# One of 31 gathered chunks of a graph layer loaded row by row by SyncE and ScalarE

## Chip, cores and metric

One core of one Trainium2 chip. The metric is the device time of one execution in microseconds, the median of three runs.

## What is computed

The input is `x`, 6250 nodes of 256 features, and 200000 edges sorted by their destination, with a weight each. A normalised `xn` goes through three branches that are summed: two graph convolution layers and a projection, a linear attention with its own feed-forward part, and then, on the sum, a mixture of eight experts of which each node takes two.

```python
def _gcn_conv(x, edge_index, edge_weight, W, b):
    deg = segment_sum(ew, col); dis = rsqrt(deg)            # with self-loops of weight 1
    h = x @ W.T
    msg = h[row] * (dis[row] * ew * dis[col])[:, None]
    return segment_sum(msg, col) + b

xn = layernorm(x)
x = x + gnn(xn, edges) + mix(xn)      # gnn: two blocks x + relu(gcn(layernorm(x))), then x @ Wp.T + bp
x = x + ffn(layernorm(x))             # 8 experts, top 2
```

What matters here is `h[row]` summed by `col`: for each destination node, the rows of `h` of all its edges' source nodes.

## The kernel before

The nodes are cut into 49 windows of 128 (`W`), the sorted edges into chunks of 128. A window needs the edges of at most a few dozen chunks; it takes 31 of its own (`OWN`), one shared with the window before it (its 31st slot is reused for that), and, in a loop whose count is only known at run time, any that are left over ("rest", about one a window). For each chunk the kernel needs two tiles: `gs[:, n, :]`, 128 rows of the table `h1_d` in HBM (layer 1) or `h2_d` (layer 2), one for each edge, at 1 KB a row; and `ss[:, slot, :]`, a 128 x 128 matrix made by VectorE that has an edge's weight in the column of its destination. The TensorE sums `ss.T @ gs` over the chunks into one PSUM bank (`acc`).

There are three stages: a preparation (degrees, normalisation, the table h1; to about 250 us in the trace), the loop of layer 1 over 49 windows (`window1` on each engine), and the loop of layer 2 (`window2`), in which the experts are computed as well. In both loops the engines run their own programs and meet at semaphores:

- GpSimd (`gathers`, `chunks`) issues one indirect DMA for each chunk (line 521). It takes 128 indices from `idx_all[:, w, n]` (partition e holds the source node of edge e) and loads the rows into `gs[:, n, :]`. Ahead of it stands a wait on `main_used` (line 520), by which the same slot's use in the window before is over. It issues `chunks(w, 8..30)`, then `chunks(w + 1, 0..7)`, then the rest of w (line 530). Each chunk has a semaphore `main_in{n}`.
- TensorE (`messages`) takes eight groups of four chunks a window (k = 0 to 7) and waits for `main_in` of each. Between the groups it does a step of the attention branch and the transposes: with k = 0 the product with `wq`, with k = 2 `nd` and a transpose of z, with k = 3 a transpose and `next_h`, with k = 4 the product with `wm`, with k = 5 a transpose, with k = 6 the 32 products of the hidden layer, with k = 7 a transpose and the product with `w2`.
- ScalarE copies what TensorE puts in PSUM back to SBUF for TensorE's next step: in order `xT` (line 646), the exponential (648), `xn_keep` (650), the weights of an expert (652), `zT` (636, `next_h`), `mT` (657), `u4` (641, `next_h_scaled`), `nT` (660), and four activations into `hT` (664).
- VectorE makes the `ss` tiles (line 1038) and does the layer norms; line 1089 is one of its once-a-window instructions.
- SyncE moves whole tiles of 128 KB: in order `ew_in` (365), `hself` (367), `u2` (369), `u1` (372), the stores of h2 (374), x1 (376) and r (384), each behind the semaphore of the instruction that it follows.

Where an engine uses a table's value as an address or a loop's bound, it reads it from SBUF into a register by `value_load` (`lookup`, line 269); before the change VectorE, TensorE and GpSimd do so.

Of the kernel before, what the change touches and what calls it, by code (L numbers as in the profile page):

```python
# [24 lines left out]
P = 128  # L25
# [9 lines left out]
S_SLOTS = 16  # L35
EARLY = (8, 16)
LO_MIN = 1
DEG = OWN + 5
PACK = 4
FRONT = 8  # L40
# [50 lines left out]
def gps_kernel(nc, x, src_cols, dst_cols, ew_cols, dst_rows, vecs, W6T, W7T, WpT, Wq, Wk, Wv, Wm, W1, W2,  # L91
               ln_cols, mix_cols, Wg, bg, eW, eb1, eb2, out):
    with ExitStack() as ctx:
# [195 lines left out]
            return lookup(eng, T_DN, w, 1, NCOL), lookup(eng, T_DBASE, w, 0, W * NCOL)  # L289

        @block.sync
        def _(sp):

# [55 lines left out]

            sp.wait_ge(s["blank_out"], 16 * 6)
            sp.wait_ge(s["kv_acc"], W)
            sp.wait_ge(s["h1_out"], 16 * (W // XG + 1))
            for b in range(2):
# [4 lines left out]
            def window1(w, last=False):  # L360
# [9 lines left out]
                sp.wait_ge(s["xn1_tp"], w + 1)  # L370
                sp.wait_ge(s["xn_kept"], w + 1)
                sp.dma_start(u1[:, :], xn_d[bass.ds(after, P), :]).then_inc(s["xn_in"], 16)
                sp.wait_ge(s["h2_done"], w + 1)
                sp.dma_start(h2_d[bass.ds(here, P), :], u4[:, :]).then_inc(s["h2_out"], 16)
                sp.wait_ge(s["x1_done"], w + 1)
                sp.dma_start(x1_d[bass.ds(here, P), :], u5[:, :]).then_inc(s["x1_out"], 16)
                if last:
# [48 lines left out]
        def _(pool):  # L426
# [82 lines left out]
            def gathers(layer, table):  # L509
                pool.wait_ge(s[f"table{layer + 1}"], 1)  # L510

                def chunks(w, some):
                    g = layer * W + w
                    for n in some:
                        if layer == 0 and n == 0:
                            pool.wait_ge(s["idx_listed"], w + 1)
                        if n == OWN - 1:
                            pool.wait_ge(s["main_used"], g * STATIC + 1 + S_SLOTS)
                        elif g:
                            pool.wait_ge(s["main_used"], (g - 1) * STATIC + n + 2 + S_SLOTS)  # L520
                        pool.indirect_dma_start(  # L521
                            gs[:, n, :], None, table[:, :],
                            bass.IndirectOffsetOnAxis(ap=idx_all[:, w, n:n + 1], axis=0),
                            element_offset=P * D).then_inc(s[f"main_in{n}"], 16)
# [23 lines left out]
        def _(act):  # L548
# [91 lines left out]
                act.wait_ge(s["h2_out"], 16 * w)  # L640
                act.activation(u4[:, :], wide(7), ACT.Copy, scale=dis[:, bass.ds(w, 1)]).then_inc(s["h2_done"], 1)

            with act.Fori(0, W) as w:
                act.wait_ge(s["xn1_tp"], w + 1)
                act.wait_ge(s["hh_ps"], w)
                act.copy(xT[:, :, :], half(5)).then_inc(s["xn1T_set"], 1)
# [1 line left out]
                act.activation(t_a[1][:, :], t_a[0][:, :], ACT.Exp).then_inc(s["q_exp"], 1)  # L648
                act.wait_ge(s["x1_done"], w)
                act.copy(xn_keep[:, :], u1[:, :]).then_inc(s["xn_kept"], 1)  # L650
                act.wait_ge(s["experts_in"], 16 * (w + 1))
                act.activation(ew_part[0][:, bass.ds(w * EW_STEP, EW_STEP)], ew_in[:, :], ACT.Copy,
                               scale=W_UP).then_inc(s["ew_high"], 1)
                next_h(w)
                act.wait_ge(s["msg_tp"], w + 1)
                act.wait_ge(s["m_ps"], w)
                act.copy(mT[:, :, :], half(5)).then_inc(s["msgT_set"], 1)
                next_h_scaled(w)
                act.wait_ge(s["mn_tp"], w + 1)
                act.copy(nT[:, :, :], half(5)).then_inc(s["mnT_set"], 1)  # L660
                act.wait_ge(s["hh_ps"], w + 1)
                act.wait_ge(s["y1_ps"], w)
                for j in range(HBLK):
                    act.activation(hT[0][:, j, :], bank[6][:, j * P:(j + 1) * P], ACT.Relu,  # L664
                                   bias=w1bias[:, j:j + 1]).then_inc(s["hr_done"], 1)
            next_h(W)
            next_h_scaled(W)

# [601 lines left out]
        def _(pe):  # L1270
# [127 lines left out]
            def messages(turn, v, k, fresh=False):  # L1398
# [1 line left out]

                pe.wait_ge(s["main_set"], v + k * U + U)
                for q in range(k * U, k * U + U):
                    if q:
                        pe.wait_ge(s[f"main_in{q - 1}"], 16 * (turn + 1))
                    mm(acc, ss[:, q % S_SLOTS, :], gs[:, q - 1 if q else OWN - 1, :], fresh and q == 0, True,
                       skip_group_check=True).then_inc(s["main_used"], 1)
# [213 lines left out]
```

## Time and profile before

| | |
|---|---|
| median of three runs | 6317.9 us (6287.8 to 6318.42) |
| span of the profiled execution | 4375.4 us |
| mean granted TensorE clock | 0.914 |
| TensorE busy | 3602.6 us, 82% |
| GpSimd busy | 3096.7 us, 71% |
| VectorE busy | 2502.6 us, 57% |
| ScalarE busy | 1195.2 us, 27% |
| indirect transfers | 3038 of `gs`, 116 of `gr` |
| moved by DMA | 515.38 MB, mean 118 GB/s |

The span runs from the first to the last instruction of one profiled execution; its durations are what the rows below give. The time of a run is not the span: 1942.5 us lie between them, and the profile has no row for these.
### The profile page before, as it was taken

Reading aid. Unit: us, or ns where it says so; the run is one execution under the profiler, and the core shown is the slowest. Engines: PE = TensorE matmul, PEld = TensorE weight load, DVE = VectorE, ACT = ScalarE, POOL = GpSimd, SP = SyncE. Lnnn points to the kernel's source line nnn. Section 1 sums busy time; section 2 is a strip of 40 time slices with the busy share of each in tenths; the row PEclk is TensorE's granted clock in tenths of the full one; section 3 lists DMA queues with packets and bytes.
Section 4 is the critical chain, followed back from the end, with each engine's and each line's share of the span. In section 5 each row is a group of like instructions: output and inputs, shape, how many; then the busy total and the mean of one; then the engine's idle time right before and its main releaser. Section 6 shows DMA issues by size and latency. Waiting matters only on the chain.

```text
span 4375.4 us, 93734 instructions
## 1 busy us (share of the span) xinstructions
PE 3602.6 (82%) x26676; PEld 3057.6 (70%) x26677; DVE 2502.6 (57%) x8948; ACT 1195.2 (27%) x3161; POOL 3096.7 (71%) x3340
## 2 busy tenths in 40 slices
PE   5976766766776776767778999999999999999989
PEld 4855655655655655655657888888888887888878
DVE  8854555554554554544555665665666565665655
ACT  2520100100110110101113444444444444444434
POOL 3357777777777777777767777777777777777772
PEclk9988888888888888888889999999999999999999
DMA  4144444444444444444433343443344343343331
GB/s 150 50 139 119 129 126 124 129 126 119 131 129 119 130 130 119 130 123 126 127 111 116 112 117 115 115 118 115 112 117 118 111 117 115 115 118 115 115 111 53
DMA packets 256046, 515.38 MB, mean 118 GB/s; under 512 B 61480, under 2 KB 154032, under 8 KB 255984
## 3 DMA queue, kind: packets, MB, share of 16 engines
q0 software_dynamic: 151392, 413.60, 33.2%
q1 hardware_dynamic: 104592, 101.17, 6.9%
q14 instruction: 49, 0.40, 0.0%
q8 instruction: 13, 0.21, 0.0%
HBM read 474.81 MB, written 39.71 MB: 118 GB/s over the span
## 4 chain that ended last, share of the span: by engine, by line
PE 48%; DVE 14%; issue 12%; POOL 11%; DMA 7%; ACT 4%; DVEq 2%; SPq 1%; POOLq 0%; ACTq 0%
PE bank L1282 46%; POOL gs L521 11%; DMA gr<-h_d,idx_r 7%; DVE ss L1038 2%; PE bank L1304 2%; ACT L696 1%; DVE rstd L717 1%; DVE rstd L715 1%; DVE rstd L716 1%; DVE st L724 1%; ACT bank L696 1%; DVEq L269 1%; DVE w L1179 1%; ACT w L699 1%; DVEq L1038 1%
## 5 line engine op out<-in xcount | busy, mean ns | idle before, releaser
L521 POOL DMA_INDIRECT gs<-h_d,idx_all x3038 | 2902.3, 955 | 957.5 <-issue 659.4
L1282 PE MATMUL bank<-gs,ss 128*128 128x256 f32 x6272 | 1601.5, 402 | 12.3 <-DMA gs<-h_d,idx_all 12.3
L1282 PEld LDWEIGHTS bank<-gs,ss 128*128 128x128 f32 x6272 | 1219.9, 202 | 191.7 <-DMA gs<-h_d,idx_all 23.2
L1038 DVE TENSOR_SCALAR ss<-iw,dst_all,ew 128x128 f32<-128x128 f32 x3152 | 882.9, 354 | 183.8 <-PE bank L1282 125.8
L696 ACT ACTIVATE bank<-bank,eb1c 128x128 f32<-128x128 f32 x1616 | 448.8, 340 | 634.3 <-PE bank L1282 633.8
L1282 PE MATMUL bank<-experts,w 128*128 128x256 f16 x4848 | 605.3, 278 | 16.8 <-DVE w L1179 16.8
L1282 PE MATMUL bank<-w,experts 128*128 128x128 f16 x9696 | 608.4, 220 | 0.0
L1282 PEld LDWEIGHTS bank<-w,experts 128*128 128x128 f16 x9696 | 569.0, 98 | 44.4 <-issue 16.6
L1282 PEld LDWEIGHTS bank<-experts,w 128*128 128x128 f16 x4848 | 468.4, 100 | 91.1 <-issue 22.1
L1282 PE MATMUL bank<-gr,sr 128*128 128x256 f32 x232 | 115.6, 593 | 479.2 <-DMA gr<-h_d,idx_r 479.2
L1179 DVE SCALAR_TENSOR_TENSOR w<-bank,w 128x512 f16<-128x512 f32 x404 | 278.3, 689 | 360.9 <-ACT w L699 360.4
L1282 PEld LDWEIGHTS bank<-gr,sr 128*128 128x128 f32 x232 | 49.2, 261 | 525.0 <-DMA gr<-h_d,idx_r 524.5
L1122 DVE SCALAR_TENSOR_TENSOR t_b<-bank,dis,vec 128x256 f32<-128x256 f32 x49 | 23.7, 484 | 490.4 <-PE bank L1282 490.4
L648 ACT ACTIVATE t_a<-t_a 128x256 f32<-128x256 f32 x49 | 20.4, 416 | 993.2 <-DVE t_a L1086 993.2
L1173 DVE SCALAR_TENSOR_TENSOR u<-bank,mask_c,u 128x256 f32<-128x256 f32 x404 | 192.9, 478 | 141.6 <-PE bank L1282 138.9
L699 ACT ACTIVATE w<-bank 128x512 f16<-128x512 f32 x404 | 241.2, 597 | 12.8
L1304 PE MATMUL bank<-ident,u 128*128 128x128 f32 x596 | 121.0, 285 | 110.1 <-DVE u L733 101.6
L530 POOL DMA_INDIRECT gr<-h_d,idx_r x116 | 112.0, 965 | 116.3 <-DVE idx_r L1045 86.7
L1304 PEld LDWEIGHTS bank<-ident,u 128*128 128x128 f32 x596 | 76.0, 142 | 167.1 <-DVE u L733 121.7
L1045 DVE COPY idx_r<-src_row 128x1 int32 x116 | 17.8, 154 | 247.2 <-PE bank L1282 208.5
L664 ACT ACTIVATE hT<-bank,w1bias 128x128 f32<-128x128 f32 x196 | 55.9, 368 | 285.3 <-PE bank L1282 285.3
L1282 PE MATMUL bank<-xT,w 128*128 128x128 f32 x784 | 126.3, 286 | 0.0
(270 smaller groups left out, 3434.1 us busy)
## 6 DMA issues: line engine op xcount, KB each, us to landing
gs<-h_d,idx_all POOLq DMA_INDIRECT x3038, 2.7
hself<-h_d SPq DMA_DIRECT2D x100, 128.0 KB, 3.2
ew_in<-in_eW SPq DMA_DIRECT2D x49, 168.0 KB, 2.6
out<-u SPq DMA_DIRECT2D x51, 128.0 KB
u<-xn_d SPq DMA_DIRECT2D x50, 128.0 KB, 3.4
h_d<-u SPq DMA_DIRECT2D x50, 128.0 KB, 1.9
u<-x_d SPq DMA_DIRECT2D x50, 128.0 KB
u<-r_d SPq DMA_DIRECT2D x50, 128.0 KB, 2.8
```

What stands on the lines that cost most here:

```text
L269: return eng.value_load(tab[0:1, row, bass.ds(w, 1)], min_val=low, max_val=high)
L521: pool.indirect_dma_start(gs[:, n, :], None, table[:, :], bass.IndirectOffsetOnAxis(ap=idx_all[:, w, n:n + 1], axis=0), element_offset=P * ...
L530: pool.indirect_dma_start(gr[:, :], None, table[:, :], bass.IndirectOffsetOnAxis(ap=idx_r[:, 0:1], axis=0), element_offset=P * D).then_inc ...
L664: act.activation(hT[0][:, j, :], bank[6][:, j * P:(j + 1) * P], ACT.Relu, bias=w1bias[:, j:j + 1]).then_inc(s["hr_done"], 1)
L696: act.activation(hid[e % 2][:, j, :], hid[e % 2][:, j, :], ACT.Gelu, scale=1.0 / (Z_UP * W_UP), bias=eb1c[:, e, j:j + 1]).then_inc(s["gelu ...
L699: act.activation(hT_part[e % 2][0][:, :, :], hid[e % 2], ACT.Copy, scale=H_UP).then_inc(s["h_high"], 1)
L715: ch.link(dve.tensor_tensor(t, y, y, ALU.mult))
L1038: m = dve.tensor_scalar(ss[:, slot + j, :], iw[:, :], dst_f[:, bass.ds(c, 1)], ew[:, bass.ds(c, 1)], ALU.is_equal, ALU.mult)
L1173: dve.scalar_tensor_tensor(out=u8[:, :], in0=wide((7, 5)[e % 2]), scalar=mask_c[:, e:e + 1], in1=u8[:, :], op0=ALU.mult, op1=ALU.add).then ...
L1179: dve.scalar_tensor_tensor(out=hT_part[e % 2][1][:, :, :], in0=hid[e % 2], scalar=H_UP, in1=hT_part[e % 2][0][:, :, :], op0=ALU.mult, op1= ...
L1282: return pe.matmul(out_ap, lhsT, rhs, start=first, stop=last, **kw)
L1304: m = pe.transpose(half(b)[:, k, :], src[:, k * P:(k + 1) * P], ident[:, :])
```

## The change

In layer 1, for each window but the first, the chunk of slot 2 (`ROWS`) is no longer gathered by GpSimd. During window w, SyncE and ScalarE load its 128 rows for window w + 1 one at a time: for each edge a register load of the source node from `idx_all`, and a direct transfer of that 1 KB row of `h1_d` into its partition of `gs`. SyncE takes partitions 0 to 63, half behind the load of `u1` and half behind the store of h2. ScalarE takes 64 to 127, sixteen each behind `xn_keep`, behind `zT`, behind `u4` and behind the four activations. Both wait first until the slot's use in window w is over. All transfers add to one semaphore, `rows_by_hand`, and TensorE waits for it ahead of the fourth message of a window. ScalarE's loop runs over 48 windows now, with the last written out behind it; both engines wait for all 49 index lists ahead of their loops.

```diff
--- before.py
+++ after.py
@@ -35,6 +35,8 @@
 S_SLOTS = 16
 EARLY = (8, 16)
 LO_MIN = 1
+ROWS = 2
+BY_SP = P // 2
 DEG = OWN + 5
 PACK = 4
 FRONT = 8
@@ -288,6 +290,12 @@
         def degree_table(eng, w):
             return lookup(eng, T_DN, w, 1, NCOL), lookup(eng, T_DBASE, w, 0, W * NCOL)
 
+
+        def row_loads(eng, w, rows_of):
+
+            for p in rows_of:
+                node = eng.value_load(idx_all[p:p + 1, bass.ds(w + 1, 1), ROWS], min_val=0, max_val=N_NODES - 1)
+                eng.dma_start(gs[p:p + 1, ROWS, :], h1_d[bass.ds(node + P, 1), :]).then_inc(s["rows_by_hand"], 16)
 
         @block.sync
         def _(sp):
@@ -350,6 +358,7 @@
 
 
             sp.wait_ge(s["blank_out"], 16 * 6)
+            sp.wait_ge(s["idx_listed"], W)
             sp.wait_ge(s["kv_acc"], W)
             sp.wait_ge(s["h1_out"], 16 * (W // XG + 1))
             for b in range(2):
@@ -370,8 +379,13 @@
                 sp.wait_ge(s["xn1_tp"], w + 1)
                 sp.wait_ge(s["xn_kept"], w + 1)
                 sp.dma_start(u1[:, :], xn_d[bass.ds(after, P), :]).then_inc(s["xn_in"], 16)
+                if not last:
+                    sp.wait_ge(s["main_used"], w * STATIC + (ROWS + 2 + S_SLOTS))
+                    row_loads(sp, w, range(0, BY_SP // 2))
                 sp.wait_ge(s["h2_done"], w + 1)
                 sp.dma_start(h2_d[bass.ds(here, P), :], u4[:, :]).then_inc(s["h2_out"], 16)
+                if not last:
+                    row_loads(sp, w, range(BY_SP // 2, BY_SP))
                 sp.wait_ge(s["x1_done"], w + 1)
                 sp.dma_start(x1_d[bass.ds(here, P), :], u5[:, :]).then_inc(s["x1_out"], 16)
                 if last:
@@ -512,6 +526,8 @@
                 def chunks(w, some):
                     g = layer * W + w
                     for n in some:
+                        if layer == 0 and w and n == ROWS:
+                            continue
                         if layer == 0 and n == 0:
                             pool.wait_ge(s["idx_listed"], w + 1)
                         if n == OWN - 1:
@@ -640,7 +656,10 @@
                 act.wait_ge(s["h2_out"], 16 * w)
                 act.activation(u4[:, :], wide(7), ACT.Copy, scale=dis[:, bass.ds(w, 1)]).then_inc(s["h2_done"], 1)
 
-            with act.Fori(0, W) as w:
+            def window1(w, last=False):
+                by_act = [range(BY_SP + i * (P - BY_SP) // 4, BY_SP + (i + 1) * (P - BY_SP) // 4) for i in range(4)]
+                if last:
+                    by_act = [()] * 4
                 act.wait_ge(s["xn1_tp"], w + 1)
                 act.wait_ge(s["hh_ps"], w)
                 act.copy(xT[:, :, :], half(5)).then_inc(s["xn1T_set"], 1)
@@ -648,14 +667,19 @@
                 act.activation(t_a[1][:, :], t_a[0][:, :], ACT.Exp).then_inc(s["q_exp"], 1)
                 act.wait_ge(s["x1_done"], w)
                 act.copy(xn_keep[:, :], u1[:, :]).then_inc(s["xn_kept"], 1)
+                if not last:
+                    act.wait_ge(s["main_used"], w * STATIC + (ROWS + 2 + S_SLOTS))
+                row_loads(act, w, by_act[0])
                 act.wait_ge(s["experts_in"], 16 * (w + 1))
                 act.activation(ew_part[0][:, bass.ds(w * EW_STEP, EW_STEP)], ew_in[:, :], ACT.Copy,
                                scale=W_UP).then_inc(s["ew_high"], 1)
                 next_h(w)
+                row_loads(act, w, by_act[1])
                 act.wait_ge(s["msg_tp"], w + 1)
                 act.wait_ge(s["m_ps"], w)
                 act.copy(mT[:, :, :], half(5)).then_inc(s["msgT_set"], 1)
                 next_h_scaled(w)
+                row_loads(act, w, by_act[2])
                 act.wait_ge(s["mn_tp"], w + 1)
                 act.copy(nT[:, :, :], half(5)).then_inc(s["mnT_set"], 1)
                 act.wait_ge(s["hh_ps"], w + 1)
@@ -663,6 +687,12 @@
                 for j in range(HBLK):
                     act.activation(hT[0][:, j, :], bank[6][:, j * P:(j + 1) * P], ACT.Relu,
                                    bias=w1bias[:, j:j + 1]).then_inc(s["hr_done"], 1)
+                row_loads(act, w, by_act[3])
+
+            act.wait_ge(s["idx_listed"], W)
+            with act.Fori(0, W - 1) as w:
+                window1(w)
+            window1(W - 1, last=True)
             next_h(W)
             next_h_scaled(W)
 
@@ -1400,7 +1430,13 @@
 
                 pe.wait_ge(s["main_set"], v + k * U + U)
                 for q in range(k * U, k * U + U):
-                    if q:
+                    if q == ROWS + 1:
+                        if not fresh:
+                            pe.wait_ge(s[f"main_in{q - 1}"], 16)
+                            pe.wait_ge(s["rows_by_hand"], 16 * P * turn)
+                        else:
+                            pe.wait_ge(s[f"main_in{q - 1}"], 16 * (turn + 2 - W))
+                    elif q:
                         pe.wait_ge(s[f"main_in{q - 1}"], 16 * (turn + 1))
                     mm(acc, ss[:, q % S_SLOTS, :], gs[:, q - 1 if q else OWN - 1, :], fresh and q == 0, True,
                        skip_group_check=True).then_inc(s["main_used"], 1)
```

## Rows read from the trace of the kernel before

**Rows 1.** The page: busy times, the slices of the span, and its gathers
```profile
span 4375.4 us, 93734 instructions
...
PE 3602.6 (82%) x26676; PEld 3057.6 (70%) x26677; DVE 2502.6 (57%) x8948; ACT 1195.2 (27%) x3161; POOL 3096.7 (71%) x3340
...
PE   5976766766776776767778999999999999999989
...
POOL 3357777777777777777767777777777777777772
...
L521 POOL DMA_INDIRECT gs<-h_d,idx_all x3038 | 2902.3, 955 | 957.5 <-issue 659.4
...
L530 POOL DMA_INDIRECT gr<-h_d,idx_r x116 | 112.0, 965 | 116.3 <-DVE idx_r L1045 86.7
```

**Rows 2.** Instructions of line 1089: min/median/max ns, first and last start us
```profile
L1089 DVE SCALAR_TENSOR_TENSOR t_b<-bank,t_a x49: 423/425/426, 262.6 to 2258.7; 128x256 f32<-128x256 f32 x49
```

**Rows 3.** Chain of waits, 1411 to 1453 us: start us, us, what
```profile
1411.26 0.94 POOL gs L521
1412.20 0.30 issue
...
1417.51 2.75 DMA gr<-h_d,idx_r
1420.31 1.23 PE bank L1282 x2
1422.58 0.60 DVE ss L1038 x2
...
1430.05 0.26 issue
...
1441.45 0.95 POOL gs L521
```

**Rows 4.** The gathers of line 521 in layer 1, and what ended their idle time
```profile
L521 POOL DMA_INDIRECT gs<-h_d,idx_all x1488: 942/946/1257, 259.7 to 2239.7; - x186
...
  issue: 305.8, 1004
  PE bank L1282: 146.8, 482
```

**Rows 5.** Busy time by engine in the loop of layer 1
```profile
core 0: us, PE busy (x) PEld busy (x) DVE busy (x) ACT busy (x) POOL busy (x), PEclk, DMA share, GB/s
262.60:2258.70 1996.10, 1426.08 (x6654) 1164.22 (x6654) 1020.45 (x4051) 202.29 (x577) 1487.78 (x1557) 0.84 0.43 125
```

**Rows 6.** SyncE's transfers in one window of layer 1: start us, us
```profile
1389.81 0.33 SPq L384 DMA_DIRECT2D r_d<-u  x1
1390.67 0.35 SPq L365 DMA_DIRECT2D ew_in<-in_eW  x1
1391.29 0.35 SPq L367 DMA_DIRECT2D hself<-h_d  x1
1391.84 0.46 SPq L369 DMA_DIRECT2D u<-in_x  x1
1392.55 0.33 SPq L372 DMA_DIRECT2D u<-xn_d  x1
1397.23 0.35 SPq L374 DMA_DIRECT2D h_d<-u  x1
1423.54 0.36 SPq L376 DMA_DIRECT2D x_d<-u  x1
```

**Rows 7.** Line 269's lookups, TensorE 1408 to 1410 us, GpSimd 51.9 to 53.5
```profile
L269 PEldq FUSED_REGOPS  x4: 51/101/156, 1408.2 to 1409.4; - x4
L269 PEldq TENSOR_LOAD <-tab x2: 300/302/305, 1408.3 to 1409.1; - x2
L269 PEldq SEQ_ASSERT  x2: 18/18/18, 1408.9 to 1409.6; - x2
...
L269 POOLq TENSOR_LOAD <-tab x2: 291/295/299, 52.0 to 52.6; - x2
```

**Rows 8.** The transfer of line 372, its register work and its landing; line 384's landing
```profile
L372 SPq DMA_DIRECT2D u<-xn_d x49: 332/333/371, 263.1 to 2259.4; - x49
L372 SPq FUSED_REGOPS  x48: 46/46/46, 262.9 to 2219.6; - x48
L372 SPq MOVE u<-xn_d x48: 29/29/29, 263.0 to 2219.7; - x48
...
DMA to landing us min/median/max: 2.5/3.4/3.8
...
DMA to landing us min/median/max: 1.8/1.9/2.0
```

**Rows 9.** A small transfer on SyncE, line 315
```profile
L315 SPq DMA_DIRECT2D eb2r<-in_eb x1: 381/381/381, 38.0 to 38.0; - x1
```

**Rows 10.** ScalarE in one window of layer 1, idle time before in brackets
```profile
1391.08 0.42 ACT L648 ACTIVATE t_a<-t_a 128x256 f32<-128x256 f32 x1 [25.19 <-DVE t_a L1086]
1391.40 0.39 ACT L650 COPY xn_keep<-u 128x256 f32<-128x256 f32 x1
1393.46 0.48 ACT L652 ACTIVATE experts<-ew_in 128x336 f32 x1 [1.67 <-DMA ew_in<-in_eW]
1393.85 0.35 ACT L636 COPY zT<-bank 128x256 f32<-128x256 f32 x1
1395.70 0.37 ACT L657 COPY mT<-bank 128x256 f32<-128x256 f32 x1 [1.50 <-PE bank L1304]
1396.74 0.47 ACT L641 ACTIVATE u<-bank,dis 128x256 f32<-128x256 f32 x1 [0.67 <-PE bank L1282]
1403.40 0.37 ACT L660 COPY nT<-bank 128x256 f32<-128x256 f32 x1 [6.19 <-PE bank L1304]
1410.36 1.14 ACT L664 ACTIVATE hT<-bank,w1bias 128x128 f32<-128x128 f32 x4 [6.59 <-PE bank L1282]
1412.31 0.37 ACT L646 COPY xT<-bank 128x256 f32<-128x256 f32 x1 [0.81 <-PE bank L1304]
```

**Rows 11.** TensorE at the start of a window of layer 1
```profile
1423.29 3.62 PE L1282 MATMUL bank<-gs,ss 128*128 128x256 f32 x8
1426.70 1.66 PE L1282 MATMUL bank<-xT,wq 128*128 128x128 f32 x8
```

## The prediction

> **What bounds the kernel now.** I read the page's busy shares first. The span has two stages with different limits: up to about half of it GpSimd is busy at seven tenths and the TensorE at six to seven, behind that the TensorE is at nine [rows 1]. The change touches the first of them, the loop over 48 of 49 windows of layer 1, so everything is read there. VectorE's instruction of line 1089 runs once a window, first at 262.6 and last at 2258.7 us [rows 2], so a window lasts (2258.7 - 262.6)/48 = 41.6 us. The chain of waits through one window [rows 3] shows what fills it: from 1411.26 the gathers follow each other at 1.25 us, 0.95 of GpSimd work and 0.30 of issue, up to the extra gather whose landing (2.75 us) frees the TensorE; behind it lies a piece over VectorE, ScalarE and TensorE, and the chain is on GpSimd again from 1441.45. In layer 1 one of these gathers waits mostly for nothing but its own issue (305.8 us in 1004 cases of 1488) and for the TensorE's use of a slot in 482 [rows 4]. 31 regular gathers and about one extra at 1.25 us are 40 us of the 41.6. So GpSimd bounds the window, with little room. ScalarE is busy 202 us of 1996 here [rows 5], and SyncE issues seven transfers a window [rows 6].
>
> **What is removed.** One gather of 31 in windows 1 to 48: 48 x (0.95 + 0.30) = 60 us of GpSimd, on its bounding path. If nothing else got slower, that is the gain; where GpSimd has its one or two waits on slots less of it shows, so 0 to 60 us.
>
> **What is added: 128 rows a window.** Each row is a register load from the index table, address arithmetic and a transfer issue, 64 on SyncE's queue and 64 on ScalarE's, and each is an in-order sequencer. No register load of either engine is in the trace; the nearest rows are the lookups of line 269. Of one lookup the parts last 0.30 us (the load), 0.15 (register operations behind it), 0.02 (the assertion) and 0.05 (those ahead of it) [rows 7]; the TensorE's two lookups begin 0.8 us apart and GpSimd's, with no address to make, 0.6 us apart (the first and last start in those rows, to a tenth) [rows 7]. For a lookup I take 0.65, between the two, as its index here needs an address too. The transfer: SyncE's dynamic ones last 0.33 us, with 0.046 and 0.029 us of register work each [rows 8], and follow each other at 0.55 to 0.62 us where nothing is waited for [rows 6]. Their rows move 128 KB instead of 1 KB, but small ones lasted no less: 0.38 us for 8 KB into 8 partitions [rows 9]. I take 0.55. A row thus costs 0.65 + 0.55 = 1.20 us of its queue. Bounds: the bare durations without gaps, 0.30 + 0.15 + 0.02 + 0.33 = 0.80; and 0.8 + 0.6 with 0.1 for two queues that issue at once, 1.50.
>
> **On ScalarE** 64 rows are 64 x 1.20 = 77 us a window, against 41.6 for the whole window now. This can't lie beside other work: the rows stand in program order ahead of ScalarE's own steps, and TensorE's next steps wait for those (zT behind the first 16 rows, mT behind the second, nT behind the third). What ScalarE adds to its 77 us:
> - its own instructions, 4.5 us [rows 10];
> - its wait between nT and the hidden layer's four activations, during which the TensorE does message groups and 32 products: 6.6 us now [rows 10]. It stays, since that work starts only with nT;
> - the wait of the next window's exponential, 25 us in the window shown [rows 10], most of it for the gathers. Afterwards TensorE stands at the fourth message of a window until all 128 rows have landed: a landing of 3.4 us after issue (a load of line 372) [rows 8], one message of 0.9 (3.62 us for four of two products each) and the product with wq, 1.66 [rows 11], and VectorE's step, 0.43 (as line 1089's) [rows 2]: 6.4 us, of which ScalarE spends 0.4 on its copy of xT, so 6.
> Its other waits (0.7 to 6.2 us today) [rows 10] are covered by the 19 us of rows ahead of each. VectorE's tail of a window, some 8 us (the chain is on it from 1422.58 to about 1430) [rows 3], lies beside the last 16 rows. Sum: 77 + 4.5 + 6.6 + 6 = 94 us. The TensorE's granted clock is 0.84 in this loop now [rows 5], and it will idle more. Some 9 us of the sum are its work; at the lower of its two levels, 1.2 GHz, throughout they could be up to twice as long. I leave that out of the sum: it is at most 48 x 9 = 430 us, and inside the bounds below.
>
> **On SyncE** the first 32 rows (38 us) start where ScalarE's first 16 do; the h2 store waits for ScalarE's second 16 (about 40 us); the other 32 rows end near 79 us, ahead of ScalarE's last 16 rows (over 80). The stores of x1 and r are queued behind those rows, and VectorE and the later layer read them only a window or more later. So SyncE is nearly as long as ScalarE, but does not set the end. If it did, the sum would be nearly the same.
>
> GpSimd with 30 x 1.25 + 1.25 = 39 us now has slack, and its saving is worth nothing. The added transfers, 128 a window, lie in a DMA system that is 0.43 busy [rows 5]; in a window twice as long the old part falls to about 0.2, so I cost them at nothing. If their landing were serial (1.9 us, the shortest kind here [rows 8]), 128 x 1.9 = 243 us a window would bound: a rival below. The new waits (SyncE's and ScalarE's for `main_used`, TensorE's for `rows_by_hand`) ask for nothing that isn't there by then, except the one counted. The unrolled code of the last window and the wait for all index lists cost once, under 2 us. Layer 2 is untouched.
>
> **The sum.** A window grows from 41.6 to 94 us: 48 x 52.4 = 2515 us, and the profiled span would go from 4375 to 6890 us. The profile stands at 4375.4 us, the runs at a median of 6317.9: 1942.5 us lie outside what the trace shows. I take that as unchanged, and get 6317.9 + 2515 = 8833, about 8830 us. With a row at 0.80 the window is 51 + 17 = 68: +1270, 7590 us. At 1.50 it is 96 + 17 = 113: +3430, 9750 us.
>
> Two pages of the Trainium skill speak against the change more strongly. "DMA: Bandwidth & Descriptors", Latency and other measured facts, gives a register load (`tensor_load`) a floor of about 600 ns. The loads in this trace take 0.30 us, so here the row decides; by the page a row would cost 1.50 us and the result would be 9750 us. The same page's Rules for kernel authors say that many small transfers should be coalesced, and that spreading transfers over several issuing engines saves only sequencer time. And "Runtime: NRT & Kernel Launch", The ~15µs preamble/postamble breakdown, allows 9 to 15 us around a kernel; by it the 1942 us are no launch cost, which feeds the first rival.
>
> **Rivals.**
> 1. The 1942 us are in the stages, not around them: the timed runs spend more on each gather than the profiled one. Spread over the 3038 + 116 = 3154 gathers [rows 1] this is 0.62 us each, a window of 41.6 + 32 x 0.62 = 61.4 us today, still GpSimd's. ScalarE's 94 us bound afterwards all the same: 48 x 32.6 = 1565, 7880 us. For it: no row explains the difference. Against: nothing in the trace shows a gather with another duration (0.94 to 1.26 us over 1488). Chance 0.25.
> 2. The rows are hidden, and it is faster. One mechanism: the sequencers overlap a load's 0.30 us and the transfer's 0.33 us with the next row's, so that a row costs little. The point from which it decides is (41.6 - 17)/64 = 0.38 us a row; below it GpSimd's 60 us come back, 6258 us. Against it: a single transfer alone lasts 0.33 and a single load 0.30, and no row shows the two overlapped on one sequencer; SyncE's transfers never begin less than 0.55 us apart [rows 6]. Chance 0.04.
> 3. As 2 but just at the limit, or GpSimd's waits on slots eat the gain: 6318 us, within 0.5%. Chance 0.02.
> 4. The row transfers land one after another, 243 us a window: +9700 us, 16000 us. Chance 0.04. It needs each transfer to wait for the last; the trace shows four transfers of SyncE in flight at once (issued 0.6 apart, one such landing after 2.5 to 3.8) [rows 6, 8].
> 5. The change does not do what it says: the diff skips the gather of chunk 2 in every window but the first and issues its rows in the 48 windows before, so I give this under 0.01.
>
> **How the numbers follow.** My forecast (ScalarE's queue bounds, a window of 68 to 113 us, the outside unchanged) has 0.65 and gives 8830 us, its own range 7590 to 9750. Rival 1 lies at 7880 with the same spread downwards (6620 at 0.80 a row: 48 x (68 - 61.4) = 317). Leaving out its lower half, rivals 2 to 4 and a little above the bound, 7500 to 9700 holds about 8 in 10. Faster by over 0.5% (about what a measurement of this kernel can tell from no change): 0.04; within 0.5%: 0.02; slower: 0.94.
>
> **What would show it.** In the profile of the changed kernel, line 1089's instruction should come every 94 us, the last at about 4.8 ms; ScalarE's sequencer should show 64 loads and 64 transfers in four blocks of 19 us each window, with a load near 0.30 and a transfer near 0.33 us; GpSimd's gathers should wait mostly for the TensorE's use of slots, and the TensorE for ScalarE's copies. The forecast is wrong in size if a row takes other than 1.2 us, wrong in kind if the gathers still follow each other at 1.25 us through the window, and wrong in its base if the span grows by 2500 us and the time does not.

## The result: 1.45 times the time

The kernel after takes 9144.5 us (median of four runs, 9123.3 to 9152.4) against 6308.6 us before (6287.8 to 6318.4): a ratio of 1.450, 95% interval 1.445 to 1.454, or 2836 us more. The profiled execution took 9142.9 us, with a span of 9141.1.

The page of the kernel after (busy times, slices, the chain's shares, its gathers), to be read beside [rows 1]:

```profile
span 9141.1 us, 136837 instructions
...
PE 4268.8 (47%) x26676; PEld 3395.7 (37%) x26677; DVE 2515.1 (28%) x8948; ACT 1188.0 (13%) x3162; POOL 3042.9 (33%) x3292
...
PE   7333323323223323233233233247777777777777
...
POOL 3222222221222222222222222235555544555443
PEclk9666666666666666666666666678888888888888
...
ACTq 42%; issue 19%; another core or an unknown queue 17%; PE 15%; ACT 5%; DVE 2%; SPq 0%; DVEq 0%; DMA 0%; POOL 0%; POOLq 0%
...
L537 POOL DMA_INDIRECT gs<-h_d,idx_all x2990 | 2846.3, 952 | 2663.0 <-PE bank L1312 1673.5
```

GpSimd fell from seven tenths to two in layer 1, and the chain that ended last lies for 42% of the span on ScalarE's sequencer, which had 0% of the chain before. VectorE's once-a-window instruction, which answers to [rows 2]:

```profile
L1119 DVE SCALAR_TENSOR_TENSOR t_b<-bank,t_a x49: 425/425/426, 261.3 to 6060.8; 128x256 f32<-128x256 f32 x49
```

A window of layer 1 lasts (6060.8 - 261.3)/48 = 120.8 us. The row blocks of ScalarE (ACTq, its sequencer) with its own instructions between them: the last block of one window and the first three of the next, which answer to [rows 10] (start us, us; idle time before in brackets):

```profile
3018.88 1.14 ACT L688 ACTIVATE hT<-bank,w1bias 128x128 f32<-128x128 f32 x4 [5.58 <-PE bank L1312]
3019.82 21.85 ACTq L298 DMA_DIRECT2D gs<-h_d  x16
3044.32 0.37 ACT L665 COPY xT<-bank 128x256 f32<-128x256 f32 x1 [24.30 <-issue]
3047.32 0.42 ACT L667 ACTIVATE t_a<-t_a 128x256 f32<-128x256 f32 x1 [2.62 <-DVE t_a L1116]
3047.64 0.39 ACT L669 COPY xn_keep<-u 128x256 f32<-128x256 f32 x1
3048.36 22.57 ACTq L298 DMA_DIRECT2D gs<-h_d  x16
3071.13 0.48 ACT L674 ACTIVATE experts<-ew_in 128x336 f32 x1 [23.10 <-issue]
3071.52 0.35 ACT L652 COPY zT<-bank 128x256 f32<-128x256 f32 x1
3072.16 21.83 ACTq L298 DMA_DIRECT2D gs<-h_d  x16
3094.09 0.37 ACT L680 COPY mT<-bank 128x256 f32<-128x256 f32 x1 [22.21 <-issue]
3094.36 0.48 ACT L657 ACTIVATE u<-bank,dis 128x256 f32<-128x256 f32 x1
3095.23 28.99 ACTq L298 DMA_DIRECT2D gs<-h_d  x15
```

Sixteen rows take about 22.5 us (16 x 1.405; the block that begins at 3095.23 takes longer, see the second effect below), and each of ScalarE's copies comes only behind them. TensorE waits for the last rows to land, and then for those copies:

```profile
3042.46 1.22 PE L1312 MATMUL bank<-gs,ss 128*128 128x256 f32 x2 [16.62 <-DMA gs<-h_d]
...
3094.51 2.07 PE L1312 MATMUL bank<-wm,mT 128*128 128x256 f32 x4 [18.33 <-ACT mT L680]
```

GpSimd in turn waits for TensorE to be done with the slots (1673.5 us in the page above). In all 48 windows ScalarE's last row is issued behind SyncE's, by 5.5 us in the mean. The register loads of the added code and its transfers (min/median/max ns; line 297 is the load, 298 the transfer; SPq rows for comparison), which answer to [rows 7, 8]:

```profile
L297 ACTq FUSED_REGOPS  x6144: 1/124/1405, 261.0 to 6054.4; - x199
...
L297 ACTq TENSOR_LOAD <-idx_all x3072: 1/447/1392, 261.1 to 6053.9; - x192
...
L297 SPq TENSOR_LOAD <-idx_all x3072: 2/427/1404, 264.1 to 6049.2; - x192
...
L298 ACTq MOVE gs<-h_d x3072: 1/29/1393, 261.9 to 6054.7; - x192
L298 ACTq DMA_DIRECT2D gs<-h_d x3072: 1/452/1402, 262.0 to 6054.8; - x192
...
L298 SPq DMA_DIRECT2D gs<-h_d x3072: 2/265/1397, 270.5 to 6050.1; - x192
```

On ScalarE a load lasts 0.447 us and a transfer 0.452; with the register work a row begins every 1.405 us (median of the 3072 starts), on SyncE every 1.26 us. The maxima of 1.4 us belong to a second effect, told below.

Busy time in the loop, which answers to [rows 5]:

```profile
core 0: us, PE busy (x) PEld busy (x) DVE busy (x) ACT busy (x) POOL busy (x), PEclk, DMA share, GB/s
261.30:6060.80 5799.50, 1739.19 (x6643) 1382.02 (x6644) 1024.28 (x4050) 196.44 (x577) 1447.83 (x1521) 0.64 0.15 44
```

One thing did not fit the sum: the span is the whole time but for 1.8 us, and layer 2, whose code is the same, now takes about 61 us a window, where the profile before has 42.

### The profile page after: what moved, and what is told of

It reads as the page before. It is cut to its first block, busy times and chain, and to the rows that moved or that the text cites. A ratio compares the mean times of both kernels' runs of the same rounds, so it can differ in the third digit from the quotient of the medians.

```text
span 9141.1 us, 136837 instructions
## 1 busy us (share of the span) xinstructions
PE 4268.8 (47%) x26676; PEld 3395.7 (37%) x26677; DVE 2515.1 (28%) x8948; ACT 1188.0 (13%) x3162; POOL 3042.9 (33%) x3292
## 3 DMA queue, kind: packets, MB, share of 16 engines
q10 hardware_dynamic: 6144, 3.16, 0.1%
## 4 chain that ended last, share of the span: by engine, by line
ACTq 42%; issue 19%; another core or an unknown queue 17%; PE 15%; ACT 5%; DVE 2%; SPq 0%; DVEq 0%; DMA 0%; POOL 0%; POOLq 0%
ACTq L297 23%; ACTq L298 18%; PE bank L1312 14%; ACT bank L726 2%; ACT w L729 1%; DVE w L1209 1%; ACT L726 1%; PE bank L1334 0%; DVE t_a L1116 0%; ACT u L657 0%; DVEq L271 0%; ACT xT L665 0%; SPq L307 0%; ACT L709 0%
## 5 line engine op out<-in xcount | busy, mean ns | idle before, releaser
L537 POOL DMA_INDIRECT gs<-h_d,idx_all x2990 | 2846.3, 952 | 2663.0 <-PE bank L1312 1673.5
L1312 PE MATMUL bank<-gs,ss 128*128 128x256 f32 x6272 | 1814.1, 436 | 1056.6 <-DMA gs<-h_d 951.2
L1312 PEld LDWEIGHTS bank<-gs,ss 128*128 128x128 f32 x6272 | 1347.9, 225 | 1333.6 <-DMA gs<-h_d 954.7
L1312 PE MATMUL bank<-experts,w 128*128 128x256 f16 x4848 | 764.4, 308 | 377.5 <-DVE w L1209 208.8
L1312 PE MATMUL bank<-xT,w 128*128 128x128 f32 x784 | 189.0, 387 | 1203.0 <-ACT nT L684 978.8
L1312 PEld LDWEIGHTS bank<-xT,w 128*128 128x128 f32 x784 | 164.9, 292 | 1222.1 <-issue 1222.0
L1312 PE MATMUL bank<-wm,mT 128*128 128x256 f32 x196 | 100.6, 667 | 853.4 <-ACT mT L680 853.4
L1312 PE MATMUL bank<-w,zT 128*128 128x256 f32 x200 | 101.7, 663 | 817.4 <-ACT zT L652 817.4
L1312 PEld LDWEIGHTS bank<-wm,mT 128*128 128x128 f32 x196 | 57.0, 321 | 885.5 <-ACT mT L680 876.7
L1312 PEld LDWEIGHTS bank<-w,zT 128*128 128x128 f32 x200 | 57.7, 318 | 837.9 <-ACT zT L652 829.2
```

Of the source, the lines that this page charges most:

```text
L537: pool.indirect_dma_start(gs[:, n, :], None, table[:, :], bass.IndirectOffsetOnAxis(ap=idx_all[:, w, n:n + 1], axis=0), element_offset=P * ...
L1312: return pe.matmul(out_ap, lhsT, rhs, start=first, stop=last, **kw)
```

## The experiments

### Where were the 1942 us? `before_again`

The kernel before, unchanged, on another chip.

> The kernel before, unchanged, for a second profile. The profile after has a span of 9141 us and a time of 9143, and its layer 2, whose code did not change, takes about 62 us a window where the profile before shows 42. Theory A (the profile before is of an execution that ran faster than the timed ones): this run has a span equal to its time, near 6300 us, with windows of about 61 us in layer 1 and 62 in layer 2. Rival B (the 1942 us lie outside the span): a span near 4375 again and a time near 6308.

It took 6228.5 us with a span of 6226.8: theory A. Its page, and line 1089:

```profile
span 6226.8 us, 93734 instructions
...
PE   6755555554555555545547777777777777777777
...
POOL 3444545545545454454544544555455454545542
...
another core or an unknown queue 34%; PE 27%; issue 16%; DVE 13%; ACT 6%; DVEq 4%; SPq 1%; DMA 0%; POOL 0%; ACTq 0%; POOLq 0%
...
L521 POOL DMA_INDIRECT gs<-h_d,idx_all x3038 | 2885.2, 950 | 1588.3 <-issue 810.1
```

```profile
L1089 DVE SCALAR_TENSOR_TENSOR t_b<-bank,t_a x49: 424/425/426, 262.6 to 3178.8; 128x256 f32<-128x256 f32 x49
```

```profile
1995.74 0.35 DVE L1038 TENSOR_SCALAR ss<-iw,dst_all,ew 128x128 f32<-128x128 f32 x1
2024.66 0.48 DVE L1122 SCALAR_TENSOR_TENSOR t_b<-bank,dis,vec 128x256 f32<-128x256 f32 x1 [28.58 <-remote]
```

```profile
2006.06 0.60 PE L1282 MATMUL bank<-gr,sr 128*128 128x256 f32 x2
2025.28 1.22 PE L1282 MATMUL bank<-hself,ident 128*128 128x256 f32 x2 [18.62 <-DVE t_b L1122]
```

TensorE's last message of the window ended at 2006.66 us. VectorE waits for nothing else here, yet it goes on at 2024.66. In the first profile this step follows the message within 0.14 us in all windows. Here it comes more than 1 us late in 38 of 48, most often by 7.1 to 7.2 us, up to 20.4.

The same mark is in the kernel after. A piece of its chain of waits, on ScalarE's sequencer in the last of the row blocks:

```profile
3112.90 0.70 ACTq L298
3113.60 0.71 issue
3114.33 0.70 ACTq L297
3115.03 0.70 issue
3115.73 0.70 ACTq L297
```

In such a stretch the sequencer goes forward in steps of 0.70 us: the register move at 3112.90 takes 0.70 us instead of 29 ns, the load at 3114.33 0.70 instead of 0.447, and 0.70 passes before the next. Not each instruction pays the same: the transfer at 3114.31 and the register operation behind it take 3 ns each, others two steps. In all, 25 instructions of ScalarE fill 19.6 us here (3112.3 to 3131.9). SyncE's sequencer goes in the same steps at the same moments: it too has instructions that start at 3114.31, 3115.72, 3117.15 and 3118.55 us. The late starts of VectorE in `before_again` lie in steps of the same size (6.44, 7.12, 7.85). So in some executions the sequencers pass through stretches in which they advance by such steps, in others they don't, and in these runs it goes by the chip. Before takes 4376.4 us on the chip of the second group of runs, 6243 on that of the first and 6321 on that of the third. The span of the profile before (4375.4 us) fits the kind without stops, the timed runs beside it the kind with them; how long that execution took as a timed run is not known.

### Does the relief of GpSimd show? `no_rows` and `no_rows_again`

```diff
 for p in rows_of:
-    node = eng.value_load(idx_all[p:p + 1, bass.ds(w + 1, 1), ROWS], ...)
-    eng.dma_start(gs[p:p + 1, ROWS, :], h1_d[bass.ds(node + P, 1), :]).then_inc(s["rows_by_hand"], 16)
+    pass
...
-pe.wait_ge(s["rows_by_hand"], 16 * P * turn)
```

> The kernel after without any row transfer or register load: chunk 2 of layer 1 is neither gathered nor loaded for windows 1 to 48, its slot keeps the rows of window 0, and the waits that guard it are gone. This is the relief of GpSimd alone. If GpSimd's gathers bound layer 1 in the timed runs, 48 x 1.25 = 60 us or more less than before: 6250 us or below. Rival (something else fills the windows of 61 us in the timed runs, such as the fetch of instructions at the end of a loop's body): within 0.5% of before, 6280 to 6340.

The waits on `main_used` that guard the rows are gone as well. 6203.5 against 6242.7 us, ratio 0.993 (0.991 to 0.996): 39 us less, under the 60 expected but clear of no change. It was repeated on a third chip:

> Chunk 2 of layer 1 neither gathered nor loaded in 48 windows (its slot keeps window 0's rows): the relief of GpSimd alone. Theory (without stops GpSimd's gathers bound the window of 41.6 us): where before takes 4376, 48 x 1.25 = 60 us less, 4316 us. Where before takes 6240 to 6310, 0.7% less, as measured there. Rival (something else is as late as GpSimd): within 0.5% of before.

6241.3 against 6320.8, 0.987 (0.985 to 0.989): 80 us less. Both chips had the stops, so neither shows what it is worth without them. But the relief is real, 39 us within the 0 to 60 of the sum and 80 us above it, even where GpSimd's gathers fill only 40 of 60 us.

### Which part of a row costs what? `loads_only`, `transfers_only`, `batched`

`loads_only` drops the transfer and TensorE's wait:

```diff
 for p in rows_of:
     node = eng.value_load(idx_all[p:p + 1, bass.ds(w + 1, 1), ROWS], ...)
-    eng.dma_start(gs[p:p + 1, ROWS, :], h1_d[bass.ds(node + P, 1), :]).then_inc(s["rows_by_hand"], 16)
...
-pe.wait_ge(s["rows_by_hand"], 16 * P * turn)
```

> Of the 128 rows a window only the register loads stay, no transfer, and TensorE does not wait for rows (slot 2 keeps the rows of window 0). Theory (a row costs its queue 1.40 us in the profile after, of which the load and its register work are 0.75 to 0.8): 64 x 0.8 = 51 us a window on each of the two queues, with some 16 us of ScalarE's other steps 67 us a window, some 6 us over the 61 of before: 6500 to 6700 us. Rival (the transfers and their landing set the time, the loads are hidden): near the time of no_rows.

`transfers_only` takes a fixed source row:

```diff
-node = eng.value_load(idx_all[p:p + 1, bass.ds(w + 1, 1), ROWS], ...)
-eng.dma_start(gs[p:p + 1, ROWS, :], h1_d[bass.ds(node + P, 1), :]).then_inc(s["rows_by_hand"], 16)
+eng.dma_start(gs[p:p + 1, ROWS, :], h1_d[P + p:P + p + 1, :]).then_inc(s["rows_by_hand"], 16)
```

> Of the 128 rows a window only the transfers stay, each with a fixed source row (so the wrong rows land in slot 2), with TensorE's wait for them. Theory (queue time): 64 x 0.5 = 32 us a window on ScalarE, with 16 to 20 us of its other steps at most 52 us, hidden in a window of 61: near 6300 us, at most 6500. Rival (landings, or two queues on one descriptor generator, set the time): most of the 2836 us stay, over 8000 us.

They took 6954.8 and 6318.3 us, beside 6242.7 of before. The load on ScalarE in the one, the transfer in the other:

```profile
L297 ACTq TENSOR_LOAD <-idx_all x3072: 3/271/712, 261.2 to 3895.8; - x192
```

```profile
L297 ACTq DMA_DIRECT2D gs<-h_d x3072: 4/265/783, 262.3 to 3241.7; - x192
```

Alone, loads follow each other at 0.61 us and last 0.271; transfers follow at 0.29 and last 0.265. The 6144 transfers of the run and their landings cost 76 us over before, 115 over `no_rows`: neither the DMA system nor two queues at once is the limit. The loads cost 751 us over `no_rows`; the 6500 to 6700 us expected would have been 300 to 500. Stops add to them: SyncE's 64 loads, 41 us at their median distance, fill 58 us of a window.

The two alone come to 0.61 + 0.29 = 0.90 us, but in the kernel after they cost 1.40. `batched` keeps both and changes only their order:

```diff
-for p in rows_of:
-    node = eng.value_load(idx_all[p:p + 1, ...], ...)
-    eng.dma_start(gs[p:p + 1, ROWS, :], h1_d[bass.ds(node + P, 1), :]).then_inc(s["rows_by_hand"], 16)
+for i in range(0, len(rows_of), 8):
+    nodes = [(p, eng.value_load(idx_all[p:p + 1, ...], ...)) for p in rows_of[i:i + 8]]
+    for p, node in nodes:
+        eng.dma_start(gs[p:p + 1, ROWS, :], h1_d[bass.ds(node + P, 1), :]).then_inc(s["rows_by_hand"], 16)
```

> The kernel after with its rows in groups of eight: eight register loads, then their eight transfers, nothing else changed. In the profile after a row takes 1.405 us of ScalarE's queue (load 0.447, transfer 0.452), while loads alone came every 0.608 us (load 0.271) and transfers alone every 0.294 us. Theory M (the alternation costs about 0.35 us a row: a load right behind a transfer waits for it and the reverse): 1.0 us a row, the window goes from 120.8 to about 95 us, 7900 us in all. Rival D (a transfer whose address is in a register costs 0.45 whatever stands before it, and the load is slow beside a busy second queue): 1.25 us a row or more, over 8600 us.

6313.9 us, on the chip without stops, so the time can't be set beside the 9144; the window and the row can. Line 1122 is here what line 1119 is above, 298 the load, 301 the transfer:

```profile
L1122 DVE SCALAR_TENSOR_TENSOR t_b<-bank,t_a x49: 424/425/426, 262.6 to 4194.7; 128x256 f32<-128x256 f32 x49
...
L298 ACTq TENSOR_LOAD <-idx_all x3072: 262/273/655, 262.3 to 4184.6; - x192
...
L301 ACTq DMA_DIRECT2D gs<-h_d x3072: 213/214/534, 267.7 to 4188.2; - x192
```

The load is back at 0.273 us and the transfer at 0.214, though its address is still in a register. A row costs 1.0 us (a load every 0.61, a transfer every 0.38) and the window is (4194.7 - 262.6)/48 = 81.9 us; `act_only` below, on the same chip and with the rows in turn, has 104.1. So theory M: on ScalarE the alternation costs 0.174 us on the load and 0.238 on the transfer. On SyncE it costs 0.164 and 0.04 (0.427 and 0.264 us in `sp_only`, 0.263 and 0.225 here). Why it does, no run shows.

### Which queue bounds? `act_only` and `sp_only`

```diff
# act_only
-row_loads(sp, w, range(0, BY_SP // 2))
-row_loads(sp, w, range(BY_SP // 2, BY_SP))
...
-pe.wait_ge(s["rows_by_hand"], 16 * P * turn)
+pe.wait_ge(s["rows_by_hand"], 16 * (P - BY_SP) * turn)
# sp_only
-if last:
+if True:
     by_act = [()] * 4
...
-pe.wait_ge(s["rows_by_hand"], 16 * P * turn)
+pe.wait_ge(s["rows_by_hand"], 16 * BY_SP * turn)
```

> Only ScalarE's 64 rows a window are loaded, SyncE's 64 are left out. Theory (ScalarE bounds; without SyncE on the same descriptor generator a row of it may cost 1.3 instead of 1.4 us): 110 to 120 us a window, 8600 to 9100 us. Rival (it takes both queues: landings or the generator bound): below 8000 us.

> Only SyncE's 64 rows a window are loaded, ScalarE's 64 are left out (those partitions of slot 2 keep window 0's rows). Theory (ScalarE's 64 rows bound the window, SyncE's lie beside them): the window is set by SyncE now, 64 x 1.15 = 74 us, five to seven transfers of its own and the landing and the first steps of the next window, 12 us together: 86 to 94 us a window, 7500 to 7900 us. Rival (SyncE's queue bounds the kernel after): over 9000 us.

Both ran on the chip without stops, beside a before of 4376.4: 7375.9 us (1.69 times) and 6806.1 us (1.56 times). `act_only`, its window, load and transfer, and then the window of `sp_only`:

```profile
L1119 DVE SCALAR_TENSOR_TENSOR t_b<-bank,t_a x49: 423/425/426, 262.0 to 5258.4; 128x256 f32<-128x256 f32 x49
...
L297 ACTq TENSOR_LOAD <-idx_all x3072: 437/447/797, 261.8 to 5251.6; - x192
...
L298 ACTq DMA_DIRECT2D gs<-h_d x3072: 450/452/528, 262.7 to 5252.4; - x192
```

```profile
L1119 DVE SCALAR_TENSOR_TENSOR t_b<-bank,t_a x49: 423/424/426, 261.4 to 4688.7; 128x256 f32<-128x256 f32 x49
```

The windows are 104.1 and 92.2 us. With the row distances in these traces they are 64 x 1.403 + 14.3 and 64 x 1.256 + 11.9. ScalarE's queue is the longer one and bounds, by 12 us. Both totals, and the window of `act_only`, lie below what was expected, which was reckoned from the profile after, with its stops; by its total `act_only` even lies where its rival was put (below 8000). The row decides against that rival: it costs 1.403 us without SyncE's rows and 1.405 with them, so no contention between the queues shows. The kernel after itself did not run on a chip without stops. From `act_only` I estimate its window there at 104.1 us or a little more, and its time at 7376 us or more.

`after_again` was meant to settle that:

> The kernel after, unchanged, beside before on this chip. On the chip of the last four runs before took 4376 us, with windows of 41.6 us in both layers and no stops of its sequencers; on the chips of the first runs it took 6240 to 6310. Theory (the added rows set the window; the stops come on top and belong to the chip, not to the change): where before takes 4376, a window of 64 x 1.405 + 15 = 105 to 108 us, 7420 to 7560 us in all. Where before takes 6240 to 6310, 9100 to 9200 again. Rival (the 120.8 us of the first profile are all rows and landings, no stops): 8150 us or more where before takes 4376.

It fell on a chip with stops: 9175.2 against 6320.8 us, ratio 1.451 (1.448 to 1.454), a repeat of the first result and no answer to the rest.

### Is there a number of rows that is hidden? `quarter`

```diff
-row_loads(sp, w, range(0, BY_SP // 2))
+row_loads(sp, w, range(0, 8))
...
-row_loads(sp, w, range(BY_SP // 2, BY_SP))
+row_loads(sp, w, range(8, 16))
...
-by_act = [range(BY_SP + i * (P - BY_SP) // 4, BY_SP + (i + 1) * (P - BY_SP) // 4) for i in range(4)]
+by_act = [range(BY_SP + 4 * i, BY_SP + 4 * i + 4) for i in range(4)]
...
-pe.wait_ge(s["rows_by_hand"], 16 * P * turn)
+pe.wait_ge(s["rows_by_hand"], 16 * 32 * turn)
```

> Of the 128 rows a window 32 are loaded, 16 on each queue (SyncE 8 + 8, ScalarE 4 x 4); the other 96 are left out. Theory (a row is hidden as long as ScalarE's queue, rows x 1.40 + 15 to 17 us, is shorter than the window, 41.6 us; with 64 rows the point is 0.38 us a row, with 1.40 us it is 18 rows): 16 x 1.40 + 16 = 38 us, hidden, so GpSimd's relief shows: 4316 to 4380 us where before takes 4376, 6180 to 6320 where it takes 6240 to 6310. Rival (rows delay the chain in proportion, at any number): a quarter of the loss, over 5000 us where before takes 4376.

6485.0 against 6320.8 us, ratio 1.026 (1.024 to 1.028), and 244 us over `no_rows_again` on the same chip: 5.1 us a window for 16 rows on each queue. The expectation of a hidden cost fell, and so did the rival, whose quarter of 2836 would be 709 us. The rows are mostly hidden but not wholly; ScalarE's rows stand in front of copies that TensorE is waiting for, and they bring 16 x 7 more instructions that can fall into a stop. In this trace ScalarE's 16 rows last 9.4 us a window beyond their median distance, so the stops are large enough to be the whole of it. Which of the two makes the 5 us stays open: that takes a chip without stops.

### What makes the stops? `before_unrolled` and `unrolled_again`

```diff
-with dve.Fori(0, W - 1) as w:
+for w in range(W - 1):
     window1(w)
```

and the same on the other three engines with a loop.

> The kernel before with its loop of layer 1 written out on all engines (49 windows, no backward branch at their ends); layer 2 and all arithmetic unchanged. In the second profile of before a window of layer 1 lasts 60.8 us, because sequencers stand still at fixed places in the code, up to 20 us at a time (VectorE's line 1122 comes 7.1 us or 13 to 20 us late in 38 of 48 windows, 0.14 us in the first profile). Theory F (the code that a backward branch leads to isn't there yet): the stops go, 42 to 46 us a window in layer 1, 5350 to 5550 us in all. Rival G (the stops come from something else, or fetching straight code costs the same): within 2% of before.

On the chip without stops: 4376.5 against 4376.4 us, and the window is the same to the tenth, (2258.4 - 261.8)/48 = 41.6 us:

```profile
L1089 DVE SCALAR_TENSOR_TENSOR t_b<-bank,t_a x49: 423/424/426, 261.8 to 2258.4; 128x256 f32<-128x256 f32 x49
```

> Layer 1's loop of before written out. On the chip without stops it took 4376.5 against 4376.4 us. On a chip with stops: theory F (they follow from the backward branch) 5350 to 5550 us; rival G (they belong to fetching any code, or to something else) within 2% of before, or slower.

On a chip with stops: 6296.4 against 6320.8 us, 0.996 (0.994 to 0.997). VectorE's step of line 1122 is late in 38 of 48 windows as before, again in steps of 0.7 us (9.21, 9.90, 10.58). Theory F falls: the stops don't follow from the backward branch, since straight code has them too. Removing 48 of them on each engine gave 24 us in all, against some 19 us of stops in each window. Nor are the stops times at which more code is loaded through the profile's instruction queue. Its row for the loop of layer 1 is the same in the first profile, without stops, and in `before_again`, with them:

```profile
q14 instruction: 20, 0.16, 0.0%
```

That is 20 packets in 48 windows, where VectorE alone is late in 38. In the kernel after, whose loop loads more code, it is 542 packets, and 542 again in `batched`, which ran without stops. What makes the stops, and what differs between the chips, is not known from these runs.

## Why the prediction was right, and where it was not

The forecast was 8830 us with a range of 7500 to 9700, slower with a chance of 0.94; it is 9144.5. The mechanism holds: ScalarE's rows stand in front of its copies and set the window. The price of a row, the other steps and the base were off, and stops that the sum did not know act on both sides of it. These errors partly cancel, and that the total came within 4% is to that extent luck.

- **GpSimd bounds the window before.** In executions without stops it does by the 41.6 us of [rows 2] and the 1.25 us of [rows 3], though no run took a gather away there. With stops it is one of several. Its relief, put at 0 to 60 us, measured 39 and 80 us.
- **The rows can't be hidden and ScalarE's queue bounds.** Shown by `act_only` (104.1 us a window) and `sp_only` (92.2), and by the chain, 42% on ScalarE's sequencer. SyncE is further behind than the text had it: 12 us a window between those two runs, 5.5 us in the kernel after.
- **The price of a row, 1.20 us.** It is 1.405 on ScalarE and 1.26 on SyncE, inside the bounds of 0.80 to 1.50. The terms that failed are the load, taken at 0.30 from other engines' lookups [rows 7] and measured at 0.447, and the transfer, taken at 0.33 from SyncE's [rows 8] and measured at 0.452 on ScalarE. `batched` shows why: no row of before had the two in turn. Register work and gaps were taken about 0.06 us too long (0.57 against 0.51). The page "DMA: Bandwidth & Descriptors" of the Trainium skill (Latency and other measured facts) gives the load a floor of about 600 ns. 0.447 and 0.271 us lie under it, so these runs don't bear that figure out as a load's duration; only the distance between two loads with their register work (0.61) is near it. The row of 1.50 us worked out with it was no further off than 1.20, but what it lacked was on the transfer's side.
- **The other steps of ScalarE's window, 17 us.** 14.3 in `act_only`. Most of the difference is the landing, put at 3.4 us behind the issue from a 128 KB transfer [rows 8]: TensorE's message starts 0.8 us behind the end of the last 0.45 us issue, 1.2 us in all. The clock that was left out of the sum fell from 0.84 to 0.64 in the loop (0.66 in `act_only`), and still did not carry these steps beyond 17.
- **The window after, 94 us.** 104.1 or a little more without stops, as 64 x 0.20 = 13 us too few for the rows are partly made up by 3 too many for the rest. With the stops that the result has, 120.8.
- **The base: 1942 us outside the span.** Wrong, and the largest error. Time and span differ by about 2 us in every run that has both. The span grew by 4766 us and the time by 2836, so the outside did not stay. The page "Runtime: NRT & Kernel Launch" of the Trainium skill (The ~15µs preamble/postamble breakdown), cited for 9 to 15 us, had pointed away from the assumption. The window before was 60.8 us in the timed executions, not 41.6. So the growth was taken from 19.2 us a window too low: 48 x 19.2 = 922 us too much. The window after was 26.8 us too short: 48 x 26.8 = 1286 us too little. Together +364 on 2515 gives 2879; the profiles show 48 x (120.8 - 60.8) = 2880, the runs 2836.
- **Rival 1** had the right place, the stages, and the wrong carrier: it laid the time on the gathers, which are as short as ever. Its 7880 us assumed the window after to be free of that time; in fact 128 rows bring some 900 more instructions a window on the two sequencers, and the stops fall on them too. Of ScalarE's 120.8 us the rows at their median distance are 90, its other steps 14, and 17 are left. The stops make nearly all of these: within the row blocks the rows are 15.8 us a window later than at 1.405 us each, against 1.3 us in `act_only`, without stops. Stops lengthen that window 1.16 times (120.8 to 104.1) and the one before 1.46 times (60.8 to 41.6).
- **Rivals 2 to 4** did not occur. 0.38 us a row, from which it would have been hidden, is not reached even by loads alone (0.61). Landings don't bound (`transfers_only`). Rival 5 did not either: the page has 2990 gathers against 3038, and 3072 rows on each queue.
- **Slips in the working.** The lower end beside rival 1 should be 6635 us, not 6620 (6317.9 + 317), and ScalarE's own instructions in [rows 10] add up to 4.4 us, not 4.5. Neither moves the forecast.

## What to carry to other kernels

One gather instruction of 1.25 us on GpSimd does the work of 128 register loads and 128 transfers: to take it off GpSimd row by row needs two queues that are free for over 60 us each, even with the loads in groups (64 x 1.0 us). When such rows stand in a queue, every copy behind them waits for all of them, so count rows x price against the window before looking at the engine's busy share, which doesn't contain a single one of them. And when a span and a time differ by more than a few microseconds, the profile is of another kind of execution than the timed ones: take a second profile before any difference is put to the edit.

## What the runs showed that was not expected

- A register load and a transfer in turn on one sequencer cost more than in groups: on ScalarE 0.447 and 0.452 us in turn, 0.273 and 0.214 in groups of eight, a row 1.40 against 1.0 us. On SyncE 0.427 and 0.264 in turn, 0.263 and 0.225 in groups.
- The same kernel (before) takes 4376 us on one chip and 6227 to 6341 us on two others and in the first runs; on one chip its runs agree within 0.5%. The difference is in stretches in which a sequencer goes forward in steps of 0.70 us; neither the backward branches nor the packets of the instruction queue (20 in the loop of layer 1 with and without stops) account for them.
